# Three edits to the order of work in a routed-experts kernel: rank products, the weights' low parts, silu's table

## The reference

```python
xn = _layernorm(x)
# s: diagonal linear recurrence over the 1024 tokens of a batch row
A = sigmoid(log_A); B_x = xn @ B_w.T + B_b      # h_t = A * h_(t-1) + B_x_t
s = h @ C_w.T + C_b
# f: the top 2 of 8 experts by a router
logits = xn @ Wr + br
weights, experts = top_k(logits, 2); weights = softmax(weights)
f = sum over the two experts of  weight * ((silu(xn @ W1[e]) * (xn @ W3[e])) @ W2[e])
out = x + s * silu(f)
```

## Time and profile before

| what | us |
|---|---|
| median of 3 runs (lowest, highest) | 799.54 (797.96, 799.91) |
| the profiled execution | 799.78 |
| its span, first to last instruction | 798.0 |
| PE busy with matmuls | 771.4 |
| DVE busy | 518.2 |
| POOL busy | 463.8 |
| ACT busy | 375.1 |

### The profile page before, as it was taken

How to read it: one execution, slowest core, us unless ns; L and a number is a source line. 1 busy time by engine, 2 the same in 40 slices (tenths; PEclk the granted TensorE clock), 3 DMA queues, 4 the chain that set the end, 5 groups by cost and what they waited for, 6 DMA issues and landing times.

```text
span 798.0 us, 17126 instructions
## 1 busy us (share of the span) xinstructions
PE 771.4 (97%) x5399; PEld 688.8 (86%) x5399; DVE 518.2 (65%) x1083; ACT 375.1 (47%) x665; POOL 463.8 (58%) x477
## 2 busy tenths in 40 slices
PE   4999989999999999999999999999999999999997
PEld 2554449999999999999999999999999999998786
DVE  6988965676777667666866564455556765552766
ACT  3975234454455345444544553445445654442530
POOL 4742847687476766856783687476547856544000
PEclk9999999999999999999999999999999999999999
DMA  9999913544565545435543644363537555943994
GB/s 291 330 302 334 131 41 107 125 77 67 127 141 113 101 81 106 68 53 135 138 70 96 165 61 79 42 145 60 112 67 192 98 128 101 329 66 40 307 373 165
DMA packets 101842, 111.02 MB, mean 139 GB/s; under 512 B 15634, under 2 KB 89236, under 8 KB 101748
## 3 DMA queue, kind: packets, MB, share of 16 engines
q0 software_dynamic: 25920, 35.54, 27.4%
q1 hardware_dynamic: 50032, 50.34, 20.3%
q10 hardware_dynamic: 25796, 24.20, 10.4%
HBM read 66.61 MB, written 43.45 MB: 138 GB/s over the span
## 4 chain that ended last, share of the span: by engine, by line
PE 84%; DVE 8%; DMA 2%; issue 2%; ACT 2%; ACTq 0%; POOL 0%; DVEq 0%; POOLq 0%; SPq 0%
PE bank L1506 15%; PE bank L1505 15%; PE bank L1507 15%; PE bank L1531 15%; PE bank L1532 7%; PE bank L1638 6%; PE bank L1494 3%; DVE xnT L1084 3%; PE bank L1406 2%; DVE stats L955 1%; PE bank L1369 1%; DVE xnT L1096 1%; PE bank L1557 1%; PE bank L1558 1%; PE bank L1556 1%
## 5 line engine op out<-in xcount | busy, mean ns | idle before, releaser
L605 POOL DMA_INDIRECT y_rows<-y_sb,token_at x128 | 215.5, 1684 | 150.8 <-DVE y_sb L1202 84.4
L1505 PE MATMUL bank<-xh,W_sb 128*128 128x256 f32 x1008 | 283.1, 281 | 1.2 <-DVE xl L1150 1.2
L1506 PE MATMUL bank<-xh,W_sb 128*128 128x256 f32 x1008 | 281.8, 280 | 0.0
L1507 PE MATMUL bank<-xl,W_sb 128*128 128x256 f32 x1008 | 281.7, 279 | 0.0
L1505 PEld LDWEIGHTS bank<-xh,W_sb 128*128 128x128 f32 x1008 | 189.2, 188 | 3.4 <-issue 1.3
L1531 PE MATMUL bank<-W_sb,hh 128*128 128x512 f32 x512 | 189.0, 408 | 0.7 <-DVE y_sb L1202 0.7
L1506 PEld LDWEIGHTS bank<-xh,W_sb 128*128 128x128 f32 x1008 | 189.4, 188 | 0.0
L1507 PEld LDWEIGHTS bank<-xl,W_sb 128*128 128x128 f32 x1008 | 188.9, 187 | 0.0
L1190 DVE TENSOR_TENSOR hbuf<-hbuf,bank 128x512 f32<-128x512 f32 x128 | 87.3, 686 | 148.8 <-PE bank L1507 129.5
L596 POOL DMA_INDIRECT xg<-xn_rows,token_at x128 | 145.3, 1136 | 37.8 <-issue 18.3
L1532 PE MATMUL bank<-W_sb,hl 128*128 128x256 f32 x512 | 143.9, 281 | 0.0
(11 more groups left out here) (253 smaller groups left out, 939.1 us busy)
## 6 DMA issues: line engine op xcount, KB each, us to landing
x_late<-L_attn_x SPq DMA_DIRECT2D x24, 512.0 KB, 9.2
raw<-L_ffn_W ACTq DMA_DIRECT2D x24, 512.0 KB
odd_raw<-L_ffn_W ACTq DMA_DIRECT2D x21, 512.0 KB
xn_rows<-h_sb SPq DMA_DIRECT2D x16, 512.0 KB, 7.4
y_rows<-xnT SPq DMA_DIRECT2D x4, 2048.0 KB, 16.2
yy<-y_rows SPq DMA_DIRECT2D x16, 512.0 KB, 9.3
out<-x_late SPq DMA_DIRECT2D x11, 512.0 KB, 6.6
x_kept<-L_attn_x SPq DMA_DIRECT2D x4, 512.0 KB, 6.9
```

What stands on the lines that cost most here:

```text
L605: return eng.indirect_dma_start(out=y_rows, out_offset=rows, in_=y, in_offset=None, bounds_check=T + TW - 1, oob_is_err=True, compute_op=A ...
L1505: eng.matmul(part, high, x_h, start=k == 0, stop=False)
L1506: eng.matmul(part, low, x_h, start=False, stop=False)
L1507: last = eng.matmul(part, high, x_l, start=False, stop=k == KD - 1)
```

## The change

Three edits, independent in the code. POOL raises `first_asked` behind the index copy of pair 1 instead of behind the DMAs of pair 0 (ahead of pair 1's DMAs). ACT does one Silu of one column (from `eps_sb`, to a place of `shift` that nobody reads any more) right behind the sigmoid. PE does the first rank product between the halves of chunk `BX_EARLY` and the second behind that chunk's second half; both halves of the next chunk follow.

```diff
@@ gather(i), POOL
                 link(eng.tensor_copy(token_at[:, 2 * i:2 * i + 2], token_idx[:, bass.ds(column, 2)]))
+                if i == 1:
+                    eng.sem_inc(first_asked, 1)
                 for t, rows in enumerate(tokens(i)):
@@ POOL's start of the gathers
             for i in range(XG_RING):
                 gather(i)
-                if i == 0:
-                    eng.sem_inc(first_asked, 1)
             rest_of_plan()
@@ ACT
                 if pos == BX_EARLY + 2:
                     eng.activation(A_sb[:, :], A_sb[:, :], ACT.Sigmoid).then_inc(A_ready, 1)
+                    eng.activation(shift[:, 0, 0:1], eps_sb[:, :], ACT.Silu)
                     eng.wait_ge(weights_ready, 1)
@@ PE
             first_groups = TILES * 3 // 4
-            make_bx(BX_EARLY)
+            bx_half(BX_EARLY, 0)
             rank(0, 0, first_groups)
-            bx_half(BX_EARLY + 1, 0)
+            bx_half(BX_EARLY, 1)
             rank(1, first_groups, TILES)
-            bx_half(BX_EARLY + 1, 1)
+            make_bx(BX_EARLY + 1)
             make_bx(BX_EARLY + 2)
```

## The result

The changed kernel took 793.91 us (median of 4, 793.66 to 794.61), beside 799.72 us for the kernel before on the same chip (4, 797.96 to 800.37): a ratio of 0.9945, 95% interval 0.9929 to 0.9961. In a second, larger set it took 795.38 us (11, 793.52 to 798.66) beside 798.43 (23, 797.73 to 802.18): 0.9960, interval 0.9946 to 0.9973. So the gain is 3 to 6 us by the medians and 3.2 to 4.4 by the ratios, where 4.1 to 4.2 was forecast; the first set's median lies 0.8 us under the stated range (794.7 to 797.6), the second's inside it. The two intervals overlap. Why medians of one kernel differ so much from set to set is the main thing learned here.

What follows compares the result with a forecast made beforehand. PE's matmul queue, busy 97% of the span, was taken to bound the kernel. Gains of 1.2 + 1.7 + 1.17 + 0.05 = 4.1 to 4.2 us from 799.78 gave 795.6 us, range 794.7 to 797.6.

Steps and rivals of the forecast that it cites:

- Part A: Weights' low parts behind pair 1's copy: first pair's second DMA undisturbed, gain 1.2 us, lower bound 0.9.
- The held DMA: Pair 1's first DMA, held by DVE's low parts, ends at 114.5 us, the second at 115.8, rows at 117.7.
- the cover of 0.3 us: Slack between pair 1's rows at 117.7 us and PE wanting them near 118.0.
- rival 2: A small cover fails: pair 1's `xl` or rows late, or table load before silu; 796.6 to 796.8 us, chance 0.12.
- Part B: PE's clock in the head holds as its idle stretch shrinks to about 1.8 us: gain 1.7 us, other bound 0.
- the nearest rows: Clock step: 1.8 us idle is nearer to 1.17 (full speed went on) than to 2.98 (it fell).
- Part C: Silu's table loaded behind the last sigmoid: PE's 1.17 us wait before the second gate product goes; other bound 0.
- Part D: Rank products 1.72 us sooner on PE; waits for `ratio_more` and the histogram leave 0.05 us, bounds 0.55 and -0.1.
- Behind the head: POOL's scatters up to 0.8 us later, y due 4 us sooner: cover expected, second scatter not held as long.
- Nothing behind it breaks: Condition for keeping to the end what is won ahead of the second pair's products; PE waits 2.6 us behind 126.
- Rival 1: The clock falls in the head all the same, leaving A + C + D = 2.4 us: 797.4 us, chance 0.16.
- Rivals 3 and 4: 3: table 0.5 to 1.7 us sooner, 793.9 to 795.1, chance 0.06; 4: POOL sets pace, 800.6 or 802.5, 0.05.

Runs made afterwards that it cites:

- part A alone: Kernel before with only the first edit, `first_asked` raised behind pair 1's index copy: 796.51 us (10 executions), ratio 0.9981.
- the tail filled: Kernel before with the second half of the fourth chunk's s made twice while PE would wait for DVE: 796.83 us, ratio 0.9978.
- part C alone: Kernel before with only the second edit, a small Silu behind the sigmoid: 795.37 us, ratio 0.9975; again on the second chip 797.05 us, 0.9980.
- part D alone: Kernel before with only the third edit, both rank products sooner in PE's order: 797.92 us (10 executions), ratio 1.000.

## Why the prediction was right, and what it missed

**Part A: right in its mechanism, mis-sized.** 1.2 us forecast with 0.9 as the lower bound; DMA and transposes gained 1.0 (114.20 to 112.94 less the 0.27 of the earlier start). The term that failed is the first DMA's 1.26: the prediction put 0.3 us of it down to DVE, and it takes 1.26 with DVE idle beside it (108.56, while the low parts start at 111.38). It is the first gather DMA's own price.

**The held DMA: wrong.** Pair 1's first DMA was to be held until both low parts had ended (114.5) and the second to end at 115.8. It ended at 113.46 and the second, undisturbed, at 114.70. The two low parts are one row with x2, and I took them for one piece of work of 2.36 us. They are two of 1.21, and the DMA is let go behind the one during which it started: 111.38 + 1.21 + 0.85 = 113.44. So the cover of 0.3 us was really more than 1, and rival 2 had less for it than I gave it.

**Part B: right in this profile, but it is a chance and not a term.** With 1.98 us of idle time (1.8 forecast) the clock held, and the product took 1.72 us. But the clock held over 2.90 in one profile and fell over 2.00 in another. The step that failed is "the nearest rows": it read the size of the idle stretch as what decides. What the change does is make a fall rarer: 1.36 falls an execution in before (37 x 2 + 39 of 83), 0.4 in after (6 in 15). 0.96 falls at 1.6 us are 1.5 us in the mean, close to the 1.7 of the sum. Filling the stretch shows that its falls come from it; that the shortening to 1.98 us is what makes them rarer is likely (part A alone has 6 falls in 10 executions), but part C's runs, which leave it as it was, have fewer than before too.

**Part C: right.** The wait of 1.17 us is gone; alone, the edit puts the second gate product at 122.59 against 123.83 in before with the tail filled, where the clock held in the head and the wait (1.14) remained. The pushed `keep_bx` cost nothing: with part C alone the histogram's copy comes at 78.83 and `token_idx` at 107.54, before at 78.81 and 107.52. Silu's small instruction comes at 70.99, right behind the load (69.70 + 1.28), and the Trainium skill's further 1.38 us (ScalarE: Activation LUTs, "What ACT_TABLE_LOAD costs") doesn't show.

**Part D: right, as good as nothing came through.** 0.05 us was forecast; `token_idx`, less the earlier start, is 0.04 us later with part D alone and in after. The two waits named took the gain; the histogram's is 0.37 us where 0.4 was forecast. That these waits are the reason is borne out by the kernels that take them away: with both gone the histogram's copy comes 1.2 us sooner than in after and the table at least 0.3, by executions that began 0.3 us later.

**Behind the head: right in outcome, one size off.** The first scatter's first DMA was 1.7 us later (142.52 to 144.22), since POOL had its plan to finish, but the next wasn't held (1.62 us and not 3.53), and the fourth `add_y` came at 159.60 with no wait of PE's (159.7 forecast). PE has one wait for `y_sb` of 1.3 us, between 420 and 440 us, where before had 0.7; in the second set's profile of after it is 0.7.

**The missed term: the tail.** "Nothing behind it breaks" was read from the waits, which showed 1.9 us, and not from the clock behind the wait. The windows over the tail, three rows, would have shown that a second 1.7 us hung on chance. The forecast of 795.6 us started from an execution with two falls, took one away and kept the other without knowing of it. That it came out 1.7 us above one median (793.91, a set with no fall in its 4 executions) and 0.2 above the other (795.38) is in part luck: which median a set shows hangs on how many of its executions have a fall. Of the 5.2 us between the profiles, 0.3 is the start, 1.0 A, 1.7 B, 1.2 C, 1.7 the tail, less 0.7 in all at PE's longer waits, for `y_sb` and at 741 us.

**Rivals.** Rival 1 (the clock falls all the same) is true of a part of the executions, not of the kernel. Rival 2 (a small cover fails) found nothing: PE has no wait between 113 and 420 us, and no load stands in front of silu. Rivals 3 and 4 fell by the rows above: `token_idx` is no sooner, and PE doesn't wait behind the head before 420 us.

## What to carry to other kernels

Where times of one kernel come in steps, sort the executions by their mean granted clock before anything is compared, and look at the clock behind every idle stretch of PE of 2 us and more, in the tail as well as where the edit is. A row with x2 or x8 is several instructions, and what waits for one of them doesn't wait for all. A product moved forward in PE's order gave nothing here until the waits in the engine behind it (DVE's, for POOL and for the histogram) were moved too.

## What the runs showed of the hardware

- **The clock's fall is a matter of the execution.** Idle stretches of 1.9 to 3.0 us, followed by dense products, let it fall in some executions and not in others: 1.91 us in the tail of before's profile, where it fell, and 1.95 in that of part D alone, where it didn't; in the head it fell behind 2.98 and 2.96 us (before, part D alone) and held over 2.90, 2.97 and 2.91 (part C alone twice, the tail filled). A fall costs 1.6 to 1.7 us in the rows, whether it shows as one product of 3.3 us or two of 2.46. The Trainium skill (TensorE: Matmul & The Clock Gate, "What's actually happening") says that the point of the clock's rise varies between executions since the chip's watching doesn't start with the kernel; the profiles agree: near the start, the eight transposes at about 17.3 us took 1.04 us in some (part A alone) and 1.92 in others (after), by where the rise fell. That is a wider spread than the 500 ns of that section: in the first the clock was up by 17.3 us, in the second it was not before 19. These transposes go with the falls: in the three profiles that fell in the head they took 1.53 to 1.92 us, in the three that held over 2.9 us 1.04 to 1.08. So where the rise falls in an execution seems to decide with the idle stretch; three against three, and no run forces it.
- **A DVE operation with two inputs from SBUF holds POOL's indirect DMA** that starts behind it until 0.82 to 0.87 us behind its own end. Five rows bear it out: in before, ends at 112.30 behind 111.45 and at 121.49 behind 120.67; in after, at 113.46 behind 112.59, at 116.65 behind 115.81 (L1248), at 120.15 behind 119.31 (the third low part). By the Trainium skill (SBUF — State Buffer, "A bandwidth-pool intuition that's wrong (but worth ruling out)") it would be some 115 ns; none of the five has so little. A DMA that began before the DVE operation, as the first one in the earlier trace rows, isn't held. Nor is one behind `x_low`, which reads one input from a bank: with the low parts later still it starts at 116.61, and the DMA of 116.71 took 0.94 us.
- **The first DMA of the first gather takes 1.26 us,** the next 0.97 where DVE holds nothing up, in every profile of this study. It isn't any pause that costs this: behind a later one of some 4 us (125.80 in after) a DMA took 1.03.
- Executions without any fall still differ by up to 1.7 us (795.32 to 797.02 with the tail filled). The two profiles of the changed kernel, 794.61 and 793.52 us, say where a part of it lies: PE's products run level from 78 to 400 us and are 1.0 us apart at 490. PE's wait for `y_sb` in between is 1.3 us in one and 0.7 in the other; the remaining 0.4 us, and why the wait differs, stay open.
